# Four graph layers on one core: in the relational reverse passes VectorE adds each window's sums onto the forward sums

## The reference, cut to what matters

```python
src2 = jnp.concatenate([src, dst]); dst2 = jnp.concatenate([dst, src])
e2 = jnp.concatenate([e, e], axis=0)
e2 = e2 / segment_sum(e2, dst2, N)[dst2]
...                                  # self edges get weight 0
def f(y): return segment_sum(y[src3] * e3, dst3, num_segments=N)
k1 = f(x); k2 = f(x + k1 / 3); k3 = f(x + (k2 - k1 / 3)); k4 = f(x + (k1 - k2 + k3))
y = x + 0.125 * (k1 + 3 * (k2 + k3) + k4)
```

## Time and profile before

| | us |
|---|---|
| time of the runs, median of 3 | 18223.73 (18201.41 to 18237.62) |
| span of the profiled execution | 18199.8 (the profile gives this execution no other time) |
| GpSimd busy | 13173.8 (72%), 13148 instructions |
| TensorE products / weight loads busy | 9887.9 (54%) / 6958.0 (38%) |
| VectorE busy | 6104.5 (34%) |
| ScalarE busy | 2627.5 (14%) |
| HBM | 63 GB/s over the span |

### The profile page before, as it was taken

How to read it: one execution, slowest core, us unless ns; L and a number is a source line. 1 busy time by engine, 2 the same in 40 slices (tenths; PEclk the granted TensorE clock), 3 DMA queues, 4 the chain that set the end, 5 groups by cost and what they waited for, 6 DMA issues and landing times.

```text
span 18199.8 us, 134071 instructions
## 1 busy us (share of the span) xinstructions
PE 9887.9 (54%) x41175; PEld 6958.0 (38%) x41175; DVE 6104.5 (34%) x10064; ACT 2627.5 (14%) x4408; POOL 13173.8 (72%) x13148
## 2 busy tenths in 40 slices
PE   6503545555558864455554555545555555549755
PEld 2303434443423353344443444334443344434443
DVE  8601111111168875222222222222222222236422
ACT  0000111111137632011111111111111111110011
POOL 5877777777777788777776777777777777760377
PEclk8655565555589987555555555555555555559755
DMA  1101121121123332111112211122122221217422
GB/s 36 22 3 49 52 51 52 52 52 52 49 64 106 105 82 61 50 53 52 53 53 55 53 53 53 53 56 53 52 53 54 54 53 53 53 55 295 183 53 57
DMA packets 591326, 1154.17 MB, mean 63 GB/s; under 512 B 256151, under 2 KB 323359, under 8 KB 564758
## 3 DMA queue, kind: packets, MB, share of 16 engines
q0 software_dynamic: 420480, 761.05, 17.1%
q1 hardware_dynamic: 166659, 383.98, 5.9%
q10 hardware_dynamic: 3600, 1.51, 0.0%
HBM read 831.58 MB, written 312.20 MB: 63 GB/s over the span
## 4 chain that ended last, share of the span: by engine, by line
POOL 71%; issue 23%; PE 4%; DVE 1%; DMA 1%; ACT 0%; POOLq 0%; SPq 0%; ACTq 0%; DVEq 0%
POOL rows L466 55%; POOL list_r L450 6%; POOL list_f L450 6%; POOL rows L477 4%; PE ps L1250 4%; PE ps L1089 0%; PE ps L1143 0%; DMA rows<-table,rows_F 0%; DVE work L1030 0%; DMA work<-in_edge_attr_4x_dram 0%; DVE work L1024 0%; DMA rows<-table,rows_R 0%; DVE work L1033 0%; PE ps L1160 0%; DMA table<-work 0%
## 5 line engine op out<-in xcount | busy, mean ns | idle before, releaser
L1143 PE MATMUL ps<-rows,onehot 128*128 128x128 f32 (+1 forms) x22880 | 5411.7, 411 | 6220.9 <-DVE rows L811 4163.4
L1143 PEld LDWEIGHTS ps<-rows,onehot 128*128 128x128 f32 x22880 | 4666.5, 301 | 7483.3 <-issue 4832.3
L466 POOL DMA_INDIRECT rows<-table,rows_F x6160 | 5921.1, 961 | 1993.7 <-issue 1873.3
L466 POOL DMA_INDIRECT rows<-table,rows_R x3520 | 3347.7, 951 | 1080.0 <-issue 1071.5
L520 ACT COPY work<-ps 128x1188 f32 x1430 | 1641.8, 1148 | 13682.6 <-PE ps L1149 13675.4
L797 DVE TENSOR_TENSOR onehot<-iota,list_F 128x512 f32<-128x512 f32 x1980 | 1285.4, 690 | 3112.1 <-ACT work L520 3112.1
L1132 PE MATMUL ps<-naught 128*128 128x396 bf16 x4290 | 1601.2, 508 | 1208.4 <-issue 1208.4
L466 POOL DMA_INDIRECT rows<-rel_table,rows_F x880 | 834.8, 949 | 1015.2 <-DMA rel_table<-list_R 747.3
L811 DVE TENSOR_TENSOR rows<-rows,list_F 128x512 f32<-128x512 f32 x880 | 616.4, 700 | 2450.2 <-DMA rows<-table,rows_F 2450.2
L811 DVE TENSOR_TENSOR rows<-rows,list_R 128x512 f32<-128x512 f32 x880 | 615.3, 699 | 2433.7 <-DMA rows<-table,rows_R 2433.7
L450 POOL DMA_INDIRECT list_r<-list_R,rows_R x850 | 1151.2, 1354 | 259.2 <-issue 259.2
(11 more groups left out here) (206 smaller groups left out, 5231.1 us busy)
## 6 DMA issues: line engine op xcount, KB each, us to landing
rel_table<-list_R SPq DMA_DIRECT2D x196, 1024.0 KB, 3.8
rows<-table,rows_F POOLq DMA_INDIRECT x6160, 2.5
gat_rows<-rows SPq DMA_DIRECT2D x220, 264.0 KB, 2.1
rows<-gat_rows SPq DMA_DIRECT2D x220, 264.0 KB
rows<-table,rows_R POOLq DMA_INDIRECT x3520, 2.5
rows<-gat_table,rows_F POOLq DMA_INDIRECT x880, 2.6
rows<-rel_table,rows_F POOLq DMA_INDIRECT x880, 2.5
list_f<-list_F,work POOLq DMA_INDIRECT x850
```

What stands on the lines that cost most here:

```text
L466: pool.indirect_dma_start(out=rows[:, t % UNROLL, 0:FEAT], out_offset=None, in_=from_table, in_offset=bass.IndirectOffsetOnAxis(ap=rows_of ...
L1143: ins = mm(into, onehot[:, s, :], rows[:, s, 0:width], start=False, stop=True, skip_group_check=True)
```

## The change

ACC_R, its stores and the additions at L1024 fall away. In a reverse pass ("adds") TensorE makes no product with the identity, and ScalarE copies nothing. Instead VectorE adds all nine slots of a window, 1188 columns out of PSUM, onto the forward sums in place (add_window): after the scaling of quad 2w it adds window w - 1, and then makes the onehots of window w + 1; the last window is added at the pass's end. The onehots wait for window_stored as before, which in a reverse pass VectorE itself now raises. TensorE waits for window_stored, two windows back, before it clears a half. VectorE loads ten window addresses every tenth window. The block columns past the last block are cleared once before the rounds, since slots past the end are now added and not overwritten. The counts of TensorE's window_summed and ScalarE skip the reverse passes (products_before).

```diff
@@ -122,9 +122,8 @@
         K = work[:, 0:BLOCKS * FEAT].rearrange("p (b f) -> p b f", f=FEAT)
-        sums_flat = {"R": work[:, 0:SUM_WORDS], "F": work[:, SUM_WORDS:]}
-        SUM_OF = {key: flat.rearrange("p (b f) -> p b f", f=AUX)[:, 0:BLOCKS, :] for key, flat in sums_flat.items()}
-        ACC, ACC_R = SUM_OF["F"], SUM_OF["R"]
+        sums_flat = work[:, SUM_WORDS:]
+        ACC = sums_flat.rearrange("p (b f) -> p b f", f=AUX)[:, 0:BLOCKS, :]
         lists = {"F": sb("list_F", [P, TILES, W]), "R": sb("list_R", [P, TILES, W])}
@@ -306,6 +305,13 @@
+        def adds(name):
+            return name.endswith(" R")
+        def products_before(name):
+            return WINDOWS * len([other for other in SUMS[:SUMS.index(name)] if not adds(other)])
         def quad_of_rows(q):
@@ -515,17 +521,17 @@
             act.sem_inc(shares_exp, 1)
-            def store_window(key, w, m0, firsts):
+            def store_window(w, m0, firsts):
                 act.wait_ge(window_summed, m0 + w + 1)
-                nc.scalar.copy(sums_flat[key][:, bass.ds(firsts[w % 10], SLOTS * AUX)].rearrange("p (k f) -> p k f", k=SLOT_BANKS),
+                nc.scalar.copy(sums_flat[:, bass.ds(firsts[w % 10], SLOTS * AUX)].rearrange("p (k f) -> p k f", k=SLOT_BANKS),
                                half_of[w % 2][:, :, 0:SLOTS * AUX // SLOT_BANKS]).then_inc(window_stored, 1)
             def store_windows(name):
-                key, m0 = name[-1], windows_before(name)
+                key, m0 = name[-1], products_before(name)
                 for w in range(WINDOWS):
                         firsts = firsts_of(mybir.EngineType.Activation, key, w, 10)
-                    store_window(key, w, m0, firsts)
+                    store_window(w, m0, firsts)
@@ -543,7 +549,7 @@
-                m0 = windows_before("gat F")
+                m0 = products_before("gat F")
                 for i in range(ITERS + 2):
@@ -556,7 +562,7 @@
                                 firsts = firsts_of(mybir.EngineType.Activation, "F", w, 10)
-                            store_window("F", w, m0, firsts)
+                            store_window(w, m0, firsts)
@@ -581,8 +587,7 @@
             for k in range(4):
-                for key in "FR":
-                    store_windows(f"rk{k} {key}")
+                store_windows(f"rk{k} F")
             root_of(3)
@@ -812,8 +817,19 @@
-                v.memset(SUM_OF[name[-1]][:, 0, :], 0.0).then_inc(sums_clear, 1)
+                if adds(name):
+                    dve.sem_inc(sums_clear, 1)
+                else:
+                    v.memset(ACC[:, 0, :], 0.0).then_inc(sums_clear, 1)
                 members_of_window(name, 0)
+            def add_window(name, w, firsts):
+                dve.wait_ge(quad_summed, quads_before(name) + 2 * w + 2)
+                if windows_before(name) + w:
+                    dve.wait_ge(window_stored, windows_before(name) + w)
+                into = sums_flat[:, bass.ds(firsts[w % 10], SLOTS * AUX)].rearrange("p (k f) -> p k f", k=SLOT_BANKS)
+                v.tensor_tensor(into, half_of[w % 2][:, :, 0:SLOTS * AUX // SLOT_BANKS], into, ALU.add).then_inc(window_stored, 1)
@@ -821,12 +837,18 @@
                 for w in range(WINDOWS):
+                    if adds(name) and w % 10 == 1:
+                        firsts = firsts_of(mybir.EngineType.DVE, name[-1], w - 1, 10)
                     if name in SCALED:
                         scale_quad(name, 2 * w, weights, aux)
+                    if adds(name) and w:
+                        add_window(name, w - 1, firsts)
                     if w + 1 < WINDOWS:
                         scale_quad(name, 2 * w + 1, weights, aux)
+                if adds(name):
+                    add_window(name, WINDOWS - 1, firsts)
                 sums_end(name)
@@ -1009,6 +1031,7 @@
+            st(v.memset(sums_flat[:, BLOCKS * AUX:], 0.0))
             for k in range(4):
@@ -1018,10 +1041,8 @@
                     block_sums(f"rk{k} {key}", weights=attr, aux=attr if k == 0 else None)
-                n = AUX if k == 0 else FEAT
                 for lo, hi in THIRDS:
                     A, count = ACC[:, lo:hi, 0:FEAT], hi - lo
-                    st(v.tensor_tensor(ACC[:, lo:hi, 0:n], ACC[:, lo:hi, 0:n], ACC_R[:, lo:hi, 0:n], ALU.add))
                     if k == 0:
@@ -1123,7 +1144,9 @@
                 if not second:
-                    if w % 2 == 0:
+                    if adds(name):
+                        pe.wait_ge(window_stored, m0 + w - 1)
+                    elif w % 2 == 0:
                         offsets["firsts"] = firsts_of(mybir.EngineType.PE, key, w, 2)
@@ -1142,11 +1165,11 @@
                 ins.then_inc(quad_summed, 1)
-                if second:
+                if second and not adds(name):
                         pe.wait_ge(window_stored, m0 + w)
-                    mm(half[:, 0:width], ident[:, :], sums_flat[key][:, bass.ds(offsets["firsts"][w % 2], width)],
+                    mm(half[:, 0:width], ident[:, :], sums_flat[:, bass.ds(offsets["firsts"][w % 2], width)],
                        start=False, stop=True, skip_group_check=True).then_inc(window_summed, 1)
```

## The result

The changed kernel takes **18270.5 us** (18267.2 to 18278.9, 10 runs) against 18224.3 (18201.4 to 18237.6, 10 runs): ratio 1.0025, 95% interval 1.0016 to 1.0034. That is 46 us slower; 18261 was forecast, with slower by more than 0.2% and no difference about even. The median lies on the slower side of that edge, but the interval (29 to 62 us) holds it.

What follows compares the result with a forecast made beforehand. GpSimd's gathers and their issue bound the passes, VectorE the stretches between; -28.6 - 0.8 + 66.4 = +37 us takes the span from 18199.8 to 18237, and with 24 us for the runs' median 18261 us; 8-in-10 range 18205 to 18310.

Steps and rivals of the forecast that it cites:

- What bounds: Whole kernel: GpSimd's gathers and their issue inside passes, 1104 us a relational pass; VectorE's chain between passes paid in full.
- Part 1: Between reverse pass and next forward pass: twelve additions of the two buffers go, 28.6 us saved over four stretches.
- the transfers, now closer together, do not queue: Between rounds: table pieces issued 4.8 us apart instead of 7.1; queueing taken as 0, 2 us at the outside.
- Part 2: Last window of each reverse pass: 1.72 us becomes 1.53 with one addition out of PSUM, 0.8 us saved over four.
- The hop: Last window: about 0.11 us from TensorE's last product to the start of VectorE's addition out of PSUM.
- Part 3: Inside reverse passes: additions free as work, but they push onehots onto gathers, each held 0.155 or 0.23 us; 66 us lost.
- A: Reverse passes: onehots miss the gathers' point, only the gain of 29 us remains, 18194 us; chance 0.12.
- B: Reverse passes: onehots start later than 0.03 us after the addition, hold grows 0.2 us, 86 in all, 18347 us; chance 0.10.
- C: Reverse passes: the addition itself holds gathers, 0.66 us in 432 windows, 285 us more, about 18510 us; chance 0.03.
- the rule behind part 3: Gathers beside onehots: a gather wants SBUF 0.12 us after its start, from 0.94 less 0.82 us.
- The upper bound of a whole onehot each: Reverse passes: if onehots start just ahead of the gathers' point, 432 holds of 0.69 us, 298 us lost.
- Rival A's second way out: Reverse passes: the first onehot would miss the gathers' point if it started 0.6 us later; A's chance 0.12.

Runs made afterwards that it cites:

- the dummy: Kernel before plus a 1188-column PSUM reduction, touching no sum, where the addition stands in reverse-pass windows but the first: 18255.8 us, 66.5 more, ratio 1.0037.
- r1_order: Changed kernel with the reverse passes' onehots directly behind the scaling, ahead of the addition: 18161.4 us, 28 less than before, ratio 0.9985.
- r10_long: Kernel before with a reduction of 1.84 us ahead of the reverse passes' onehots, where gathers set the pass: 18191.2 us, 3 more, ratio 1.0002.
- r2_psum_iota: Changed kernel in its own order, reverse-pass onehots reading their row of numbers from PSUM: 18153.8 us, 35 less than before, ratio 0.9980.
- r11_mid: Kernel before with a reduction of 1444 columns (about 1.65 us) ahead of the reverse passes' onehots: 165.8 us more, ratio 1.0091.
- r12_longer: Kernel before with a reduction of 2.04 us ahead of the reverse passes' onehots, on a third chip: 224.8 us more, ratio 1.0126.
- r5_short: Kernel before with a reduction of 906 columns (about 1.09 us) ahead of the reverse passes' onehots, on the 20108.5 us chip: 5 us less.
- r7_longer: Kernel before with a reduction of 1816 columns (about 2.04 us) ahead of the reverse passes' onehots, on the 20108.5 us chip: 9 us less.

## Why the prediction was right

- **What bounds**: GpSimd's gathers in the passes and VectorE between the rounds. Right: the chain is unchanged, what was taken from VectorE between rounds came back in full (29.5 us in the traces), and what was added to it inside the passes did not count as work.
- **Part 1**, 28.6 us saved by the additions: 29.4 measured alone (13 to 45). That the transfers, now closer together, do not queue was right too: from the last H addition's start to the first gather it is 7.56 us (11905.72 to 11913.28), as before (11863.57 to 11871.13).
- **Part 2**, the last window: 1.39 us for 1188 columns out of PSUM from a straight line; 1.383 on the median. The hop was 0.15 instead of 0.11 in the stretch shown, and so 0.14 instead of 0.19 us saved there. The estimate from the Trainium skill (VectorE: DVE Perf Modes, errata section), 65 ns more for a PSUM operand, is not borne out here.
- **Part 3**, no scaling late: right, VectorE waits about 4.3 and 1.8 us for rows in a window of rounds 1 to 3. The loss, 66 us: 66.5 with the dummy (42 to 93), and 62 us of holds in the traces of the changed kernel, where the other 11 of the 73 us are gathers that are all 3 ns longer. Every eighth gather is held 0.21 us in rk0 R (0.21 to 0.23 forecast) and 0.14 to 0.15 in the others (0.14 to 0.155).
- **Rivals**: A (the onehots miss the gathers) did not come by itself; it is what r1_order makes of the kernel, 28 us below before where A had 29. B and C did not come: the onehots start 0.03 us after the addition, and of 436 gathers begun in the midst of an addition none is held.
- **The number**: 18261 forecast, 18270 measured. The 9 us between them are inside the interval of the difference (29 to 62 us, 37 forecast), and no term of the sum is shown to be off by them.
- **A step that was right by luck of place**: the rule behind part 3, that a gather wants SBUF 0.12 us after its start. For a onehot that starts well before the gather it gives the same hold as what the runs show, so the forecast stood; for one that starts level with the gather it is wrong (r10_long). The upper bound of a whole onehot each, 298 us, is not reached by this hold either: the longest in a relational pass is 0.52 us on the chips where gathers set the pass. Rival A's second way out was mis-sized for the same reason: 0.45 us later, not 0.6, is enough.
- The Trainium skill (SBUF — State Buffer, "Who interferes with whom") infers that tensor_tensor doesn't hold descriptor generation. The changed kernel against r1_order and r2_psum_iota shows that it holds GpSimd's indirect gather when both its inputs are in SBUF; that a tensor_tensor with one PSUM input doesn't is as the same section says. Which part of the gather is held is not shown: its indices are read from SBUF (rows_R), and the same section has two SBUF inputs contend with a GpSimd instruction that reads SBUF.

## What to carry to other kernels

Where GpSimd's indirect transfers set the pace, look at the mean of a gather pass by pass, not at VectorE's share: 20 ns more on 880 gathers is 18 us a pass, and which VectorE instruction does it shows in the gather that ends a fixed time after it (here 0.82 us). Either give the instructions with two SBUF operands a place between two gather starts, or move one operand to PSUM, which here was worth more (138 us with both) than the change under study lost. And a stretch in which the bound engine stands still is paid one to one: work moved out of it into covered time is a gain only as long as what it pushes aside has room.

## What the runs showed of the hardware that was not expected

- A gather is held by a onehot that started 0.56 to 0.05 us before it, for (onehot's start - gather's start) + 0.565 us, within some 0.01 us. One that starts less than 0.03 us before it, or level with it, does not hold it and is itself stretched instead, by 0.07 us where it started 0.03 us before (r10_long, r11_mid).
- The hold isn't monotone in the shift, and a held gather can shift the next ones so that the scaling, harmless until then, holds one too (r12_longer).
- One chip ran the same kernel in 20108 us instead of 18189, with engines standing still for up to some 10 us at a time, and there the holds cost nothing (r5_short to r7_longer: 3 to 9 us less than before, no difference).
